# Weighing of two experts' results moved into the stage that follows

## What is computed

```python
# layer 0, 16 sequences x 256 tokens x 128 features; ln = layer norm
x = x + diff_attention(ln(x))            # A1
x = x + experts_gelu(ln(x))              # F1
x = x + causal_attention(ln(x))          # A2, 16 heads
x = x + experts_gelu(ln(x))              # F2
# layer 1
x = x + single_head_attention(ln(x))     # A3
x = x + expert_layer(ln(x))              # A4 (16-head attention), F3 (swiglu experts)
x = x + recurrence_layer(ln(x))          # RI, RR, RM
x = x + expert_layer(ln(x))              # A5, F4

# what an expert stage adds (gelu form; no biases in the swiglu form, whose two
# weights are a softmax over the two best probabilities)
expert_values, expert_indices = jax.lax.top_k(router_probs, k=TOP_K)     # TOP_K = 2
expert_values = expert_values / (jnp.sum(expert_values, axis=-1, keepdims=True) + 1e-09)
...
weights_E = (one_hot * expert_values[..., None]).sum(axis=2)
moe_out = jnp.einsum('bse,bsed->bsd', weights_E, all_outputs)
return x + _mlp(x, sh_w1, sh_b1, sh_w2, sh_b2) + moe_out
```

## Time and profile before

| | us |
|---|---|
| median of 3 runs | 3139.07 (3137.94 to 3140.11) |
| the profiled execution's own time | 3138.48 |
| its span | 3136.7 |
| PE busy | 2609.3 (83%) |
| PEld busy | 2112.4 (67%) |
| DVE busy | 2131.1 (68%) |
| ACT busy | 1510.0 (48%) |
| POOL busy | 1116.1 (36%) |

### The profile page before, as it was taken

One profiled execution on the slowest core, in us unless ns is written; L12 is line 12 of the kernel. 1 busy time (PEld: TensorE's weight loads), 2 busy tenths in 40 slices (PEclk: granted clock), 3 DMA queues, 4 the chain that ended last, 5 costly groups with the idle time before them and its releaser, 6 DMA issues. The chain is left out here.

```text
span 3136.7 us, 66606 instructions
## 1 busy us (share of the span) xinstructions
PE 2609.3 (83%) x19422; PEld 2112.4 (67%) x19422; DVE 2131.1 (68%) x5674; ACT 1510.0 (48%) x3156; POOL 1116.1 (36%) x2202
## 2 busy tenths in 40 slices
PE   0999999779849999789479999789467679998794
PEld 0787878559848888579467777569223457776594
DVE  2888888652278888532578888655667588886655
ACT  0555555325426666345246777323146247775131
POOL 2222323264422111555232333466311333332753
PEclk9999999899969999899789999889678879998897
DMA  7111111212221011322201111223200011102134
GB/s 277 42 33 33 37 33 37 82 57 67 67 56 27 23 25 25 98 63 71 70 4 28 27 27 27 66 65 92 63 6 0 5 25 27 27 24 58 56 88 118
DMA packets 166298, 161.04 MB, mean 51 GB/s; under 512 B 30407, under 2 KB 130773, under 8 KB 164112
## 3 DMA queue, kind: packets, MB, share of 16 engines
q1 hardware_dynamic: 145680, 106.88, 13.4%
q0 software_dynamic: 18176, 34.67, 3.5%
q10 hardware_dynamic: 2304, 17.83, 1.3%
HBM read 60.17 MB, written 58.20 MB: 38 GB/s over the span
## 5 line engine op out<-in xcount | busy, mean ns | idle before, releaser
L1193 DVE TENSOR_REDUCE A_mx<-A_s 128x2 f32<-128x512 f32 x1056 | 715.2, 685 | 155.6 <-PE A_s L1376 148.8
L1026 ACT ACTIVATE A_Pm<-A_t 128x384 f32<-128x384 f32 (+1 forms) x1024 | 557.3, 544 | 239.5 <-PE A_t L1392 217.2
L1376 PE MATMUL A_s<-A_KB,A_Q 128*128 128x128 f32 (+1 forms) x2112 | 502.8, 321 | 7.2 <-DVE A_mx L1193 3.0
L1392 PE MATMUL A_t<-A_Q,A_KB 128*128 128x256 f32 (+1 forms) x2048 | 423.1, 288 | 0.0
L235 POOL DMA_INDIRECT ybuf<-F_yo,F_idx x312 | 307.9, 987 | 252.0 <-DVE F_yo L453 134.3
L963 POOL TENSOR_TENSOR A_mh<-A_mx,A_nil 128x8 fp32r<-128x8 f32 x260 | 58.1, 223 | 910.1 <-DVE A_mx L1193 907.2
L1376 PEld LDWEIGHTS A_s<-A_KB,A_Q 128*128 128x128 f32 x2112 | 329.2, 196 | 46.7 <-DVE A_mx L1193 29.9
L1392 PEld LDWEIGHTS A_t<-A_Q,A_KB 128*128 128x128 f32 x2048 | 318.6, 193 | 0.4 <-issue 0.4
L225 POOL DMA_INDIRECT xbuf<-xs,F_dst x256 | 249.0, 973 | 143.9 <-issue 75.0
L588 PE MATMUL F_hb<-F_xT,F_wt 128*128 128x256 f32 x1248 | 298.4, 382 | 0.2 <-DVE F_wt L463 0.2
L1404 PE MATMUL A_ot<-A_Pm,A_V 128*32 128x256 f32 (+3 forms) x3640 | 293.1, 386 | 1.9 <-ACT A_O L1040 1.9
(11 more groups left out here) (385 smaller groups left out, 5787.9 us busy)
## 6 DMA issues: line engine op xcount, KB each, us to landing
A_KB<-A_kst SPq DMA_DIRECT2D x408, 64.0 KB, 2.0
F_xr<-xbuf SPq DMA_DIRECT2D x156, 136.0 KB, 2.2
xbuf<-zero ACTq DMA_DIRECT2D x16, 1088.0 KB, 18.4
A_KB<-A_kst SPq DMA_DIRECT2D x136, 128.0 KB, 2.3
xs<-ybuf SPq DMA_DIRECT2D x32, 512.0 KB, 6.9
ybuf<-F_yo,F_idx POOLq DMA_INDIRECT x312, 2.3
F_WA<-in_L_ffn_ew SPq DMA_DIRECT2D x2, 2048.0 KB, 8.7
F_WA<-in_L_ffn_ew SPq DMA_DIRECT2D x16, 256.0 KB, 5.4
```

Of the source, the lines that this page charges most:

```text
L1026: act.activation(Pm[r][:, j, :], tbank[j % 2][:, 0:PW], ACT.Exp, scale=SCALE).then_inc(t_free, 1)
L1193: dve.reduce_max(mx[r][:, :, j], sbank[use_ % SB][:, :].rearrange("p (t k) -> p t k", t=TPS), AX).then_inc(s_free, 1)
L1376: last = pe.matmul(o[:, t * SEQ:t * SEQ + nk], Q1[q][:, c0 + t * P:c0 + (t + 1) * P], KB[q][:, j % HPT, c0:c0 + nk], start=not masked, sto ...
L1392: last = pe.matmul(o[:, t * SEQ:(t + 1) * SEQ - q0], KB[q][:, j % HPT, c0 + t * P:c0 + (t + 1) * P], Q2[g % 2][:, c2 + q0:c2 + SEQ], start ...
```

## The change

- **Weighing.** It leaves the expert stages. Their SP no longer waits for `back` and loads nothing of YBUF. The loads, the wait before them and the additions stand in the next stage, by a new class `Returns`. A2: DVE adds sequences 0 and 1 in the lead-in, where statistics, root and norm of sequence 0 now come last; POOL adds the others in the loop (`add_beside`, two multiplications and two additions of 128 x 256), after the maxima of the first group of each sequence. A3: DVE adds each sequence ahead of its statistics in `norm(b)`. RI: DVE adds each block of four tiles (for each expert) in `stat(b)`. Store: DVE adds five tiles of each quarter's eight, POOL three, and each quarter is stored by itself.
- **Token weights.** ACT's exponentials and DVE's chain L487 to L497 stand ahead of the tile loop.
- **Bias.** The eight additions of `b2` stand in the first eight tiles of the loop.
- **Buffers.** `xs` and W are padded by four tiles; W, `yo` and `idx` are global, since the writes that read `yo` and `idx` now outlive their stage. `zero` is gone: XBUF is cleared from `xs[0]` by eight transfers of twice the size.
- **POOL's loop** in A2 is written out, 16 sequences in a row, in place of the hardware loop. The other attention stages keep it.

```diff
 # sparse_expert_stage, SP
-            for q in range(4):
-                if q == 0:
-                    for r in range(RING):
-                        sp.wait_ge(back[r], 32 * (NTILE // RING))
-                    sp.wait_ge(sh_added, NBLK * (2 if gelu else 1))
-                for c in range(2):
...
-                    sp.dma_start(xs[c][:, q * 8:(q + 1) * 8, 0:D], src).then_inc(returned[q], 16)
...
+            sp.wait_ge(sh_added, NBLK * (2 if gelu else 1))
 # ACT: moved ahead of the tile loop
+            act.wait_ge(route_step, NBLK * 16)
+            act.activation(l2[:, :, :], l2[:, :, :], ACT.Exp)
+            act.activation(e2[:, :], d2[:, :], ACT.Exp).then_inc(ex_ready, 1)
...
 # DVE: the chain ch(...) of reduce_sum to W1_ moved ahead of the first fetch; in the loop
+                if gelu and k < NBLK:
+                    dve.tensor_tensor(XB[:, k + 1, :, :], XB[:, k + 1, :, :], b2[:, :].unsqueeze(1).to_broadcast([P, TPB, D]), ALU.add)
             result(LAST)
...
-            for q in range(4):
-                dve.wait_ge(returned[q], 32)
-                for c, wc in enumerate((W0, W1_)):
-                    for t in range(q * 8, (q + 1) * 8):
-                        last = dve.scalar_tensor_tensor(X[:, PAD + t, :], xs[c][:, t, 0:D], wc[:, t:t + 1], X[:, PAD + t, :], ALU.mult, ALU.add)
-                    ch(last)
...
+class Returns:
...
+    def load(self, sp):
+        for s, n in self.G["returns"]:
+            sp.wait_ge(s, n)
+        for q in range(4):
+            for c in range(2):
+                rows = self.G["YBUF"][c * NTOK + q * NTOK // 4:c * NTOK + (q + 1) * NTOK // 4, :]
+                sp.dma_start(self.G["xs"][c][:, q * 8:(q + 1) * 8, 0:D], rows.rearrange("(t p) d -> p t d", p=P)).then_inc(self.returned[q], 16)
+
+    def add(self, dve, b):
...
+        for c in range(2):
...
+            if c == 1:
+                dve.wait_ge(self.half_added, b + 1)
+            for t in range(lot):
+                x = X[:, b + PAD // lot, t, :]
+                last = dve.scalar_tensor_tensor(x, ys[:, b, t, 0:D], wc[:, b, t:t + 1], x, ALU.mult, ALU.add)
+            last.then_inc(self.x_final if c else self.half_added, 1)
+
+    def add_beside(self, pool, b, first, weighed, weighed_ready, pool_added):
...
+        pool.wait_ge(self.x_final, b)
+        for c in range(2):
...
+            last = pool.tensor_tensor(weighed[:, c, :, :], ys[:, b, :, 0:D], wc[:, b, :].unsqueeze(2).to_broadcast([P, lot, D]), ALU.mult)
+        last.then_inc(weighed_ready, 1)
+        pool.wait_ge(weighed_ready, b - first + 1)
+        x = X[:, b + PAD // lot, :, :]
+        pool.tensor_tensor(x, x, weighed[:, 0, :, :], ALU.add).then_inc(pool_added, 1)
+        pool.wait_ge(pool_added, b - first + 1)
+        pool.tensor_tensor(x, x, weighed[:, 1, :, :], ALU.add).then_inc(self.x_final, 1)
 # init_globals
+    part = NTT * ROWW
+    zero = G["xs"][0][:, 0:NTT, :].rearrange("p t c -> p (t c)")
 # attention_stage (back is set in A2 alone), POOL's loop
                     maxima(b * NQ + g + 1, (g + 1) % 2)
+                    if g == 0 and back:
+                        back.add_beside(pool, b + 2, 2, weighed, weighed_ready, pool_added)
                     if g == 1:
                         root(b + 2)
 # attention_stage, DVE, end of the lead-in
+            if back:
+                dve.wait_ge(back.returned[0], 32)
+                back.add(dve, 0)
+                back.add(dve, 1)
+                stat(0)
+                norm(0)
+                norm2(0)
             dve.memset(credit[:, 13:14], 0.0).then_inc(started, 1)
 # single_head_stage, DVE
             def norm(b):
+                back.add(dve, b)
+                dve.wait_ge(back.x_final, b + 1)
+                dve.memset(spare_x[:, :], 0.0)
 # recurrence_in_stage, DVE
             def stat(b):
...
+                back.add(dve, b)
+                dve.wait_ge(back.x_final, b + 1)
+                dve.memset(spare_x[:, :], 0.0)
 # store
-            sp.dma_start(out.rearrange("(t p) d -> p t d", p=P), G["X"][:, PAD:NT - PAD, :]).then_inc(stored, 16)
...
+            for q in range(4):
+                sp.wait_ge(added, q + 1)
+                sp.wait_ge(pool_added, q + 1)
+                sp.dma_start(OUT[:, q * 8:(q + 1) * 8, :], X[:, PAD + q * 8:PAD + (q + 1) * 8, :]).then_inc(stored, 16)
```

More of the change, by code:

```diff
@@ L276, in _ @@
                     copied(b + 2)
+            act.wait_ge(route_step, NBLK * 16)
+            act.activation(l2[:, :, :], l2[:, :, :], ACT.Exp)
+            act.activation(e2[:, :], d2[:, :], ACT.Exp).then_inc(ex_ready, 1)
+            if not gelu:
+                act.wait_ge(fx_ready, 1)
+                act.activation(e2[:, :], d2[:, :], ACT.Exp).then_inc(ex_ready, 1)
             def tile_turned(k, q):
@@ L467, in _ @@
                 dve.memset(G["Y"][:, NT - PAD:NT, :], 0.0)
+            ch = Chain(dve, w_step, 0)
+            dve.wait_ge(ex_ready, 1)
+            ch(dve.reduce_sum(S[:, :], l2[:, :, :], AX))
+            if gelu:
+                ch(dve.scalar_tensor_tensor(den[:, :], S[:, :], 1e-9, e2[:, :], ALU.mult, ALU.add))
+            else:
+                ch(dve.reciprocal(den[:, :], S[:, :]))
+                dve.scalar_tensor_tensor(d2[:, :], e2[:, :], 1.0, den[:, :], ALU.subtract, ALU.mult).then_inc(fx_ready, 1)
+                dve.wait_ge(ex_ready, 2)
+                ch(dve.tensor_copy(den[:, :], e2[:, :]))
+            ch(dve.tensor_scalar(S[:, :], den[:, :], 1.0, None, ALU.add))
+            ch(dve.reciprocal(W0, S[:, :]))
+            ch(dve.tensor_tensor(W1_, e2[:, :], W0, ALU.mult))
             dve.wait_ge(experts_in, NEXP)
@@ L666, in _ @@
             for c in range(2):
-                last = dve.memset(xs[c][:, :, D:ROWW], 0.0)
+                dve.memset(G["W"][c][:, NTT:], 0.0)
+                last = dve.memset(xs[c][:, :, :], 0.0)
             last.then_inc(padded, 1)
@@ L698, in store, with add @@
     stored = st.sem("stored")
+    returned, half_added, pool_half = [st.sem(f"S_returned{q}") for q in range(4)], st.sem("S_half_added"), st.sem("S_pool_half")
+    added, pool_added = st.sem("S_added"), st.sem("S_pool_added")
+    X, xs, W, YBUF = G["X"], G["xs"], G["W"], G["YBUF"]
+    OUT = out.rearrange("(t p) d -> p t d", p=P)
+    weighed = st.sb("S_weighed", [P, 2, 3, D])
+    def add(dve, q, c):
+        for t in range(q * 8, q * 8 + 5):
+            last = dve.scalar_tensor_tensor(X[:, PAD + t, :], xs[c][:, t, 0:D], W[c][:, t:t + 1], X[:, PAD + t, :], ALU.mult, ALU.add)
+        return last
     with nc.Block() as block:
@@ L948, in _ @@
             pool.wait_ge(c_pool, 5)
-            root(0)
+            if not back:
+                root(0)
             pool.memset(KB[0][:, :, :].bitcast(F32), 0.0).then_inc(cleared, 1)
@@ L978, in _, with sequence @@
             root(1)
+            if back:
+                for q in range(1, 4):
+                    pool.wait_ge(back.returned[q], 32)
             maxima(0, 0)
-            with pool.Fori(0, NSEQ) as b:
+            def sequence(b):
                 for g in range(NQ):
                     maxima(b * NQ + g + 1, (g + 1) % 2)
+                    if g == 0 and back:
+                        back.add_beside(pool, b + 2, 2, weighed, weighed_ready, pool_added)
                     if g == 1:
@@ L991, in _ @@
                     pool.tensor_tensor(XS[:, b + S0 - 1, :, :], XS[:, b + S0 - 1, :, :], YS[:, b + S0 - 1, :, :], ALU.add)
+            if back:
+                for b in range(NSEQ):
+                    sequence(b)
+            else:
+                with pool.Fori(0, NSEQ) as b:
+                    sequence(b)
             if diff:
@@ L1641, in _ @@
             norm2(2)
+            for q in range(1, 4):
+                dve.wait_ge(back.returned[q], 32)
             def step(b, p, ahead=2):
@@ L1791, in stat @@
             def stat(b):
+                if isinstance(b, int) and b % 2 == 0:
+                    for q in ([0] if b == 0 else [1, 2, 3] if b == 2 else []):
+                        dve.wait_ge(back.returned[q], 32)
+                back.add(dve, b)
+                dve.wait_ge(back.x_final, b + 1)
+                dve.memset(spare_x[:, :], 0.0)
                 for t in range(TPB):
```

120 lines of the change are left out of this document (75 added, 45 removed).

## The result

| | us |
|---|---|
| before, 8 runs beside the changed kernel | 3138.85 (3137.76 to 3140.74) |
| changed, 8 runs | 3148.30 (3146.67 to 3149.26) |
| ratio | 1.003, 95% interval 1.0021 to 1.0039 |
| the changed kernel's profiled execution, its span | 3148.31, 3146.3 |

The account below looks back on a forecast made before the run. It named no whole-kernel bound, only expert-stage tails where one engine works and the others wait. Terms -19.4 - 10.0 + 4.4 + 6.1 + 1.0 = -17.9 from 3138.5 gave 3120.6, forecast 3120.5 us; range 3104 to 3134.

Parts of the forecast that it names:

- The stage starts: F1, F2 and F3 close at POOL's last issue plus 1.2 us: 25.1, 24.8 and 24.8 us earlier.
- Rival (e): Stages close only when the row writes have landed, 3 x 1.3 us: 3124.5 us; chance 0.06.
- Bias and weights: Bias hidden in F1's and F2's tiles, freeing 0.5 us each; weights' chain adds 2.4 us in F3 and F4.
- A2: Lead-in 20.8 us (+4.3), POOL's loop additions hidden, table loads +1.9; with F1's earlier close -19.4 us.
- rival (b): In A2's lead-in POOL's memsets don't hold the casts: 7 us less, 3113.5 us; chance 0.08.
- A3: First results at +9.2 (+3.3), DVE's additions lengthen the period by 0.7, 12.0 in all; with F2's close -10.0 us.
- RI: First results +6.8, DVE's additions stand in the chain, 2.5 a block, +20.0; with F3's close and chain +4.4 us.
- Store: DVE's and POOL's additions exclude each other and add to 27.5 us: +3.7, with F4's chain +6.1 us.
- rival (a): DVE and POOL work side by side in the store stage: 11.1 us less, 3109.5 us; chance 0.20.
- Init and A1: With larger clears, earlier issue may win 2 us and delayed small loads may lose 5; taken as +1 us.
- rival (c): PE loses its clock in A3: 18 us more, 3138.5 us, no visible change; chance 0.11.
- (d): POOL's additions in A2 become the bound: 3146 us or more; chance 0.05.

Follow-up runs that it names:

- the last kernel: Changed kernel with half the loads in tails, swiglu weights behind tiles, store on DVE alone, RI additions one block ahead, clears behind A1's small loads: 3081.32 us, ratio 0.9824.

## Why the prediction was wrong

**The stage starts: this step failed.** "After the change a stage closes at POOL's last issue plus 1.2 us." The 1.2 us were read at the end of a stage whose last engine was DVE, with POOL long done; I carried them over to a stage whose last engine is POOL. There 7.47 us pass. 7.5 - 1.2 = 6.3 us, in F1, F2 and F3, and in F4, where SP issues its loads 7.5 us after the last write (3113.45 against 3105.91) instead of 1.3: 25.1 us in all, nearly the 27.5 between the forecast and the result. That the rest comes to so little is chance: beside the 6.3 us, the forecast was 4 us too low in the row of A3 and in that of RI, and 2, 4 and 2 us too high in the rows of A2, the store and init, and these nearly cancel. Rival (e) had the right kind of cause, a close later than the last issue, with the wrong event behind it (the rows' landing) and 1.3 us as its price.

**Bias and weights.** The bias was hidden, as said; but the 0.5 us that it should free at the end of F1 and F2 didn't show in full: the last issue did shrink from 1.50 to 0.98 us, but it began 0.3 (F1) and 1.1 us (F2) later in its stage, so F1's ended 0.2 us earlier and F2's 0.6 later. The weights' chain was mis-sized: 2.4 us for each swiglu stage, where the first tile came 6.0 (F3) and 4.0 us (F4) later. ACT's table was counted as going "in a place where it has nothing else to do", and its reload stands in the first tile, 1.28 us. 2.0 of F3's 6.0 us arise earlier, in the routing, which the change doesn't touch; 1.8 of them were there in the last kernel too, and their cause is open.

**A2** was right: lead-in 19.9 us (862.71 to 882.64) against 20.8, casts held as said (rival (b) is out), POOL's operations 0.61 to 0.75 us and hidden. The eight table loads came; A2 grew by 4.2 us, of which the lead-in is 3.4, so 0.8 us at most is theirs, where 1.9 were taken.

**A3.** The period was right (+0.76 us, +0.7 said). The first results came at +11.3 instead of +9.2: SP reached the loads at +4.0, and the first quarter took 7.35 us. +18.5 instead of +15.3.

**RI** was right in size and in its reason: 27.3 us (26.8 said), and the run that moves the additions into the wait shows that they stood in the chain. The forecast took the 2.5 us a block as the place's price; it is the order's, and I should have asked whether another order is free.

**Store.** That the engines hold each other up was right, rival (a) is out. But the two times aren't added in full: in the 16.0 us in which POOL runs, DVE gets 19 of its 40 additions through, most of them one to a POOL operation, so 21.95 us instead of 27.5. With the load (6.8 instead of 6.1) and the last store (3.2 instead of 3.9) this is -5.5, and hides part of the DRAIN in this term.

**Init and A1**: a 9.2 us shorter init gained only 0.6 us, and the last kernel shows that A1's small loads were indeed behind the clears.

**PE's clock** stayed at 1.00 in A3 though its share fell from 99% to 87% (34.77 of 40 us), so rival (c) is out; (d) is out by the 3.16 us that POOL still waits:

```profile
1560.00:1600.00 40.00, 34.77 (x215) 28.00 (x214) 35.57 (x150) 22.26 (x65) 7.66 (x17) 1.00 0.00 0
```

The range failed because the stage's close was taken as known, with no bound from above: the four tails share that term, so its error counts four times. (The two upper bounds that the range names, 8.4 and 4 us, lead from 3120.5 to 3132.9 and not to 3134; the result is beyond either.)

## What to carry to other kernels

When a tail is taken away, list everything that ran beneath it, queue instructions like DRAIN too, which stand in no busy time: the next latest of them sets the gain. Work moved to another stage is free only in a wait of the engine that gets it; if it lands in a chain, look for a place one step earlier in the same loop before giving up on the move. Price moves one by one, since one of four here gained 0.6% and the four together lost 0.3%.

## What the runs showed of the hardware

- POOL's DRAIN ended 6.44 us after POOL's last write at the end of each stage with indirect writes, took 6.43 us when all the rows had landed before it (6425 to 6431 ns), and 0.8 to 1.5 us in the attention stages.
- An engine that only issues transfers can hold a stage: eight loads of 512 KB kept SP for 10.96 us, four for 3.83.
- Two small loads kept SP for 17.17 us while large transfers of another queue were under way, and for 0.94 us without them.
- DVE's additions from SBUF beside POOL's operations from SBUF took up to 1147 ns instead of 337; 64 on DVE alone (17.39 us) were faster than 40 with POOL's help (21.95 us).
